# Eight edits to a four-block network kernel: opening, position rounds, band, group norm, one drain

## The reference

```python
# block 0: attention in 14 x 14 windows with relative positions, then an MLP
qkv = win.reshape(Bw, N, C) @ qkv_w + qkv_b              # q, k, v, 12 heads of 16
attn = einsum('bqc,bkc->bqk', q * scale, k)
rel_h = einsum('bhwc,hkc->bhwk', r_q, rel_pos_h[idx])    # the position rounds
rel_w = einsum('bhwc,wkc->bhwk', r_q, rel_pos_w[idx])
out = softmax(attn + rel_h + rel_w) @ v @ proj_w + proj_b
x = x + out; x = x + gelu(_ln(x) @ fc1_w + fc1_b) @ fc2_w + fc2_b
# block 1: group norm, then a Fourier mixer
g = x.reshape(B, H, W, 32, C // 32)
m, s = mean(g, (1, 2, 4)), var(g, (1, 2, 4)); v = (g - m) / sqrt(s + 1e-5)
x = x + irfft2(softshrink(softshrink(rfft2(v) * w1 + b1) * w2 + b2)) + v
# block 2: landmark attention with a 33-tap convolution of v along the tokens,
#          then each token through 2 of 8 experts
# block 3: full attention, then each token through 1 of 8 experts
```

## Time and profile before

| | us |
|---|---|
| runs shown | 1159.53, 1156.06, 1154.65; median 1156.06 |
| profiled execution | 1155.44 |
| its span | 1153.6, mean granted TensorE clock 0.913 |
| PE busy | 998.3 (87%) |
| PE weight loads | 757.4 (66%) |
| DVE, ACT, POOL busy | 578.9, 420.4, 286.6 |

### The profile page before, as it was taken

One profiled execution on the slowest core, in us unless ns is written; L12 is line 12 of the kernel. 1 busy time (PEld: TensorE's weight loads), 2 busy tenths in 40 slices (PEclk: granted clock), 3 DMA queues, 4 the chain that ended last, 5 costly groups with the idle time before them and its releaser, 6 DMA issues. The chain is left out here.

```text
span 1153.6 us, 20446 instructions
## 1 busy us (share of the span) xinstructions
PE 998.3 (87%) x7506; PEld 757.4 (66%) x7507; DVE 578.9 (50%) x1394; ACT 420.4 (36%) x853; POOL 286.6 (25%) x399
## 2 busy tenths in 40 slices
PE   6896999999699699899799839999929789993996
PEld 5685778787466488688699715666727545562775
DVE  3754554653311376465575654444448477844221
ACT  3665054546232133244352101111107356651332
POOL 4464320110100112100000262555422311103242
PEclk9885899999799899899998859999969899995899
DMA  8444863330002120200003711111133433415660
GB/s 92 118 120 122 163 159 81 81 82 2 1 28 71 43 63 2 55 1 1 2 1 84 227 34 30 49 48 49 40 109 90 124 118 99 141 54 173 201 204 15
DMA packets 103318, 91.58 MB, mean 79 GB/s; under 512 B 25905, under 2 KB 95095, under 8 KB 102590
## 3 DMA queue, kind: packets, MB, share of 16 engines
q1 hardware_dynamic: 93161, 77.15, 25.3%
q0 software_dynamic: 5632, 11.07, 3.6%
q10 hardware_dynamic: 4437, 2.17, 0.7%
HBM read 64.44 MB, written 29.70 MB: 82 GB/s over the span
## 5 line engine op out<-in xcount | busy, mean ns | idle before, releaser
L1305 DVE TENSOR_REDUCE l0a_nmax<-l0a_psS 98x2 f32<-98x392 f32 x96 | 54.4, 567 | 54.8 <-PE l0a_psS L1120 50.7
L2743 ACT ACTIVATE l2e_H<-l2e_psH 128x512 f32<-128x512 f32 x40 | 21.7, 594 | 130.2 <-PE l2e_psH L2705 130.2
L895 ACT ACTIVATE l3a_PT<-l3a_psST 128x512 f32<-128x512 f32 x96 | 54.6, 595 | 32.2 <-PE l3a_psST L806 31.4
L1255 ACT ACTIVATE l0a_PT<-l0a_psST 98x392 f32<-98x392 f32 x96 | 47.2, 497 | 42.2 <-PE l0a_psST L1162 41.9
L2723 PEld LDWEIGHTS l2e_psY<-W2T,l2e_HT 128*128 128x128 f32 x320 | 51.5, 190 | 15.9 <-issue 15.8
L2666 POOL DMA_INDIRECT ys<-l2e_Y,result_of x40 | 42.0, 1049 | 72.3 <-DVE l2e_Y L2770 66.2
L2723 PE MATMUL l2e_psY<-W2T,l2e_HT 128*128 x320 | 57.3, 332 | 1.3 <-DVE l2e_Y L2770 0.8
L941 DVE TENSOR_REDUCE l3a_nmax<-l3a_psS 128x2 f32<-128x512 f32 x48 | 33.0, 687 | 25.2 <-PE l3a_psS L776 25.2
L2770 DVE COPY l2e_Y<-l2e_psY 128x384 f32<-128x384 f32 x20 | 11.2, 558 | 65.2 <-PE l2e_psY L2723 65.2
L2702 PE MATMUL l2e_psH<-W1T,l2e_XT 128*128 x80 | 41.3, 640 | 2.7 <-issue 2.0
L2661 POOL DMA_INDIRECT l2e_X<-xn,token_at x40 | 39.3, 981 | 17.1 <-issue 17.1
(11 more groups left out here) (570 smaller groups left out, 2739.6 us busy)
## 6 DMA issues: line engine op xcount, KB each, us to landing
l3w_A<-in_w SPq DMA_DIRECT2D x8, 771.0 KB, 4.6
l3w_B<-in_w SPq DMA_DIRECT2D x8, 672.0 KB, 5.4
l3a_QS<-qd SPq DMA_DIRECT2D x72, 64.0 KB, 2.2
l3a_KS<-kd SPq DMA_DIRECT2D x72, 64.0 KB, 2.3
rd<-l0q_r_p SPq DMA_DIRECT2D x24, 168.0 KB
l0a_QS<-qd SPq DMA_DIRECT2D x54, 64.0 KB
l0a_KS<-kd SPq DMA_DIRECT2D x54, 64.0 KB
W2T<-in_w2t SPq DMA_DIRECT2D x2, 1536.0 KB, 16.7
```

Source lines behind the costliest of these rows:

```text
L895: nc.scalar.activation(PT[n % 3][:, s, :], psST[item % 2][:, :], ACT.Exp).then_inc(exp_done, 1)
L1255: ex = nc.scalar.activation(PT[n % 3][0:WQ, s, :], psST[item % 2][0:WQ, 0:2 * W0], ACT.Exp)
L1305: mx = nc.vector.tensor_reduce(nmax[k % 2][0:WQ, 2 * j:2 * (j + 1), s], psS[item % 2][0:WQ, 0:2 * W0].rearrange("p (t k) -> p t k", t=2), ...
```

## The change

1. Opening: the clearing of `band` and the scatter leave SP's stream for window attention's (after load(4) and load(5)); the six reads of `kb` go from ahead of image 0 to behind image 2.
2. Position rounds: ACT and DVE empty the banks of round r + 1 before they split round r.
3. The position rows of the first group are loaded in the opening.
4. The six products of window attention's start go; three like them stand at the end of the opening, behind the last second piece.
5. Group norm of the first pair: computed inside the MLP by a new `FourierFront`, with the weights of the Fourier mixer loaded at the MLP's start, constant rows behind p = 0, negation behind p = 1, total to square at p = 2, and variance to norm at p = 3.
6. The two-expert block ends without GpSimd's drain; its input semaphores move to the stage around it.

```diff
-    def block(self):
-        return self.ctx.enter_context(self.nc.Block())
+    def block(self, drained=True):
+        return self.ctx.enter_context(self.nc.Block(no_gpsimd_drain=not drained))
 ...
             # opening, SP
             sp.dma_start(rows(G["kbd"], ...), kbp[:, :, :], ...).then_inc(kb_out, 16)
-            sp.dma_start(rows(G["band"], 0, [P * TW, NH], ...), rows(consts["zeros"], ...)).then_inc(band_out, 16)
             sp.dma_start(KOH[:, :], consts["koh"]).then_inc(first_in, 16)
             sp.dma_start(RS[RR:RM, :, :], rows(consts["winrows"], ...)).then_inc(first_in, 16)
-            sp.wait_ge(kb_out, 16)
-            for t, piece in enumerate(K_TERM):
-                sp.dma_start(kb[t * HD:(t + 1) * HD, :], rows(G["kbd"], ...), ...).then_inc(kb_in, 16)
             for i in range(B):
                 for pieces, dst in ((qp, G["qd"]), (kp, G["kd"])):
                     pieces.sync(sp, rows(dst, ...), i, i % 2)
-                if i == 0:
-                    sp.wait_ge(rev_done, 1)
-                    sp.wait_ge(band_out, 16)
-                    sp.dma_start(rows(G["band"], 0, [P * TW, NH], [TW + 1, P], [1, TAPS]), free(backwards[:, 0:1], ...)).then_inc(band_out, 16)
+                if i == 2:
+                    sp.wait_ge(kb_out, 16)
+                    for t, piece in enumerate(K_TERM):
+                        sp.dma_start(kb[t * HD:(t + 1) * HD, :], rows(G["kbd"], ...), ...).then_inc(kb_in, 16)
 ...
                     rp.sync_each(sp, to, *piece_of(r, u))
+                    if (r, u) == (2, 0):
+                        sp.wait_ge(rp.out[0], 2 * rp.unit)
+                        sp.wait_ge(rp.out[2], 2 * rp.unit)
+                        position_rows(sp, G, RS, 0, first_in)
             # opening, TensorE, after the rounds
+            pe.wait_ge(rp.p1, FOURS * len(rounds))
+            for c in range(3):
+                nc.tensor.matmul(psR[:, :], G["ident"][0:CH, :], QF[:, 0, c * 2 * T:(c + 1) * 2 * T], start=True, stop=True)
             # opening, ACT (DVE alike, with its own banks)
-            for r, a, axis in rounds:
+            def relative_out(r, a, axis):
                 if r >= 2:
                     act.wait_ge(rp.rest, FOURS * (r - 1))
                 for bank in (0, 2):
                     act.wait_ge(full[bank], r + 1)
                     evacuate_rel(...).then_inc(emptied[bank], 1)
+            relative_out(*rounds[0])
+            for r, a, axis in rounds:
+                if r + 1 < len(rounds):
+                    relative_out(*rounds[r + 1])
                 ready = [(emptied[bank], r + 1) for bank in range(5)]
                 for u in range(FOURS):
                     rp.scalar(nc, act, columns(axis, u), *piece_of(r, u), *(ready if u == 0 else ()))
 ...
             # window attention, SP and TensorE
-                sp.dma_start(RS[slot][0:RR, :, :], rows(G["rd"], ...)).then_inc(stack_in[slot], 16)
                 if k:
+                    position_rows(sp, G, RS[slot], k, stack_in[slot])
 ...
+                if k == ring:
+                    sp.dma_start(rows(G["band"], ...), rows(G["consts"]["zeros"], ...)).then_inc(band_out, 16)
+                if k == ring + 1:
+                    sp.wait_ge(band_out, 16)
+                    sp.dma_start(rows(G["band"], ...), free(G["backwards"][:, 0:1], ...)).then_inc(band_out, 16)
             early.finish(sp)
+            sp.wait_ge(band_out, 32)
 ...
-            for c in range(6):
-                nc.tensor.matmul(psS[0][:, :], G["ident"][0:CH, :], G["QF"][...], start=True, stop=True)
 ...
             # l0_mlp: SP, POOL, TensorE, ACT, DVE
+            gn.load_weights(sp, w_next)
+            gn.clear_weights()
+                if p == 1:
+                    gn.negate_weights(pool)
+                if p == NP - 2:
+                    pe.wait_ge(xT_done, 2 * NP)
+                    gn.mean(pe, psT[0], 0)
+                if p == NP - 1:
+                    gn.variance(pe, psT[1], 0)
                 second(p)
+                if p == NP - 2:
+                    gn.square(act, 0)
+                    gn.square(act, 1)
+            gn.root(act, 0)
+                if p == NP - 2:
+                    gn.total(dve, 0, (x_in, 16))
+                    gn.centre(dve, psT[0], 0)
+                if p == NP - 1:
+                    gn.square_total(dve, 0)
+                    gn.with_eps(dve, psT[1], 0)
+                    gn.scale(dve, 0)
+                    gn.norm(dve, 0)
+                if p == 0:
+                    gn.constant_rows()
 ...
             # experts_any
-        x_in = [st.sem(f"x_in{r}") for r in range(RING)]
-        y_out = rows_out
+        x_in, y_out = rows_in, rows_out
-        block = st.block()
+        block = st.block(drained=False)
```

More of the change, by code:

```diff
@@ L382, in _ @@
                     pieces.sync(sp, rows(dst, i // 2 * 3 * C * 2 * T + i % 2 * T, [2 * T, CH], [2 * C * T, 3], [2 * CH * T, 2], [1, T]), i, i % 2)
-                if i == 0:
-                    sp.wait_ge(rev_done, 1)
-                    sp.wait_ge(band_out, 16)
-                    sp.dma_start(rows(G["band"], 0, [P * TW, NH], [TW + 1, P], [1, TAPS]), free(backwards[:, 0:1], [0, P], [1, TAPS])).then_inc(band_out, 16)
+                if i == 2:
+                    sp.wait_ge(kb_out, 16)
+                    for t, piece in enumerate(K_TERM):
+                        sp.dma_start(kb[t * HD:(t + 1) * HD, :], rows(G["kbd"], piece * C, [1, HD], [HD, NH]), allow_slow_non_contiguous=True).then_inc(kb_in, 16)
             qp.finish(sp)
@@ L1108, in score @@
                 q_, k_, r_, ps = QS[k % ring][0:SR], KS[k % ring][0:SR], RS[k % ring], psS[item % 2]
[L1109 to L1110 removed]
+                if j == 0 and s == 0 and k:
+                    pe.wait_ge(stack_in[k % ring], 13 * 16 * (k // ring + (1 if k % ring else 0)))
                     if k == 1:
@@ L1648, in backward @@
                 mm.then_inc(y_mm, 1)
-            mean(0)
-            variance(0)
             for p in range(NP):
@@ L1655, in _ @@
                 if p + 1 < NP:
-                    mean(p + 1)
+                    gn.mean(pe, psM, p + 1)
                 first(2 * p)
@@ L1730, in centre @@
-            def centre(p):
-                dve.wait_ge(mean_mm, p + 1)
-                for u in range(2):
-                    V.tensor_tensor(in_groups(XC[u][:]), in_groups(X(2 * p + u)), spread(psM[:, u * GROUPS:u * GROUPS + 1]), ALU.subtract).then_inc(xc_done, 1)
-            def square_total(p):
-                if p:
-                    dve.wait_ge(var_mm, p)
-                for u in range(2):
-                    dve.wait_ge(sq_done, 2 * p + u + 1)
-                    V.tensor_reduce(squares[:, u, :], by_group(SQ[u][:, 0, 0:1]), AX.XY, ALU.add).then_inc(square_done, 1)
@@ L1758, in norm @@
-            def norm(p):
-                for u in range(2):
-                    i = 2 * p + u
-                    if p:
-                        dve.wait_ge(f_mm, 2 * i - 2)
-                        dve.wait_ge(xs_done, i - 1)
-                    V.tensor_tensor(in_groups(XN[u][:]), in_groups(XC[u][:]), spread(rstd[:, u, 0:1]), ALU.mult).then_inc(xn_done, 1)
             def hidden(i, a):
@@ L1812, in _ @@
                 if p + 1 < NP:
-                    total(p + 1)
-                    centre(p + 1)
-                    square_total(p + 1)
+                    gn.total(dve, p + 1, *([(x_in, 16)] if p + 1 == NP - 1 else []))
+                    gn.centre(dve, psM, p + 1)
+                    gn.square_total(dve, p + 1)
                 hidden(2 * p, 0)
@@ L3296, in build @@
         net.window_attention()
-        net.window_mlp()
-        net.fourier()
+        with Stage(nc, "l1g") as across:
+            gn = FourierFront(across, net.G)
+            net.window_mlp(gn)
+            net.fourier(gn)
         net.landmark_attention()
         with Stage(nc, "l2y") as between:
-            rows_out = [between.sem(f"rows_out{r}") for r in range(RING)]
-            net.two_experts(rows_out)
+            rows_in, rows_out = ([between.sem(f"{name}{r}") for r in range(RING)] for name in ("rows_in", "rows_out"))
+            net.two_experts(rows_in, rows_out)
             with Stage(nc, "l3f") as across:
```

241 lines of the change are left out of this document (130 added, 111 removed).

## The result

| | median us | executions | ratio to before, 95% interval |
|---|---|---|---|
| before | 1156.58 | 1154.65 to 1159.53 (4) | |
| changed kernel | 1168.90 | 1166.17 to 1174.91 (4) | 1.0117 [1.0089, 1.0145] |

A forecast was written before the change was run, and what follows sets the result against it. TensorE, busy 998.3 of 1153.6 us, was taken as the bound, through earlier starts or full clock. Six terms summed to −18.5 us from 1155.44, giving 1136.9, then 1137.5 against the runs' median; range 1127 to 1147.

The forecast's parts named there:

- The start of window attention: Window attention: without six products scores start with the stage, group 1 waits for copies to about 8.9 us; −6.4 us.
- Rival (d): Window attention: cold TensorE start, first groups wait on and off, clock stays at half; 1167.5 us, slower; 4%.
- rival (a): Position rounds: new order costs nothing, as TensorE keeps full clock and pieces overlap; 1132 us; 15%.
- The images: Opening: band transfers and kb copies no longer delay qd, so the slow image pair becomes like the fast one; −7.7 us.
- The rounds: Position rounds: round 2's units wait behind VectorE's round 3 copies, and piece 7 for piece 4's buffer; +7.4 us.
- The band in window attention: Window attention: clearing of band holds SP's queue, so load(5) lands after its scores are due; +3 us.
- Rival (c): Window attention: band transfers hold loads by the full +8 us and the clock falls in that wait; 1144.5 us; 12%.
- The group norm: MLP and Fourier stage: first pair's norm moves into the MLP, so forward products start sooner and run faster; −9.8 us.
- The drain: End of two-expert stage: without GpSimd's drain the barrier waits only for the last indirect transfer's issue; −5.0 us.
- Rival (b): After the two-expert stage: drain only moves, as the next stage's reads of ys wait for the same transfers; 1142.5 us; 10%.

The follow-up runs named there:

- e5: e3 with six products instead of three at the opening's end and none at window attention's start: 1143.04, 1156.31, 1168.40 and 1174.72 us.
- e2: The kernel before without its six products at window attention's start, nothing else: 1180.97, 1191.17, 1207.78 and 1210.05 us beside 1155.24.
- e1: The changed kernel with the six products put back at window attention's start: 1142.87 us beside 1155.24, ratio 0.9890.
- e3: e1 with the old order of the position rounds (banks emptied right before the round is split): 1133.58 us beside 1155.24, ratio 0.9828.
- e4: The changed kernel with only the old order of the position rounds, still without the six products: 1165.23 and 1165.68 us beside 1155.24.
- e7: e3 without the three products at the opening's end, six kept at window attention's start: 1132.75 us beside 1154.91.
- e12: e3 with the six reads of kb back ahead of image 0, band transfers still in window attention: 1143.23 us beside 1157.31.
- e15: e3 with the clearing of band and the scatter in the opening instead of window attention: 1142.86 us beside 1155.75.
- e18: e16 with the clearing of band and the scatter behind window attention's last load too: median 1132.31 us beside 1156.15.
- e9: e5 with three products added at the start of window attention: 1130.15 to 1158.09 us, median 1146.85, beside 1157.31.
- e10: e5 with three products added at the wait for group 1's copies: 1134.82 to 1144.87 us, median 1137.86, beside 1157.31.
- e8: e3 with GpSimd's drain back at the end of the two-expert block: 1140.10 us beside 1154.91.
- e16: e10 with the sixteen weight and constant transfers behind window attention's last load instead of load(3): 1130.34 us beside 1156.15, ratio 0.9775.
- e13: e10 with the sixteen weight and constant transfers behind load(5) instead of load(3): 1147.28 us beside 1155.75.

## Why the prediction was wrong, step by step

The predicted 1137.5 us was missed by 31.4. Five of the six terms came within 3 us of the traces; the sixth turned a gain of 6.4 into a loss of 27.7.

- **The start of window attention (−6.4): the step that failed.** It took the six products for 8.3 us of work that nobody reads, let "up to a quarter more for a cold clock" hide in the wait for group 1's copies, and went on at full clock behind it. In the changed kernel group 0 took 13.1 us at half clock (120.30 to 133.36) instead of 7.0, with no wait in it to hide in. Where the stage did start at full clock (e5), group 1's scores began 9.8 us behind its start, near the 8.9 of the term: what failed is the clock, not the copies. The runs show that the scores and products of this stage, at half clock, need not raise it at all: 85.7 us in the changed kernel, at least 120 in e2, while TensorE is busy without a break. The same instructions at full clock keep it (e1, e3). The six products are what carries TensorE from the one to the other. The three products left in the opening do not. In the changed kernel they ran at half clock to their end and 2.9 us of idle time followed; in e4 the clock rose within them and was lost again over 3.7 us of idle time; beside the six they change nothing (e7).
- **Rival (d) is what happened, in the main.** A cold start and a clock that stays at half, in this stage and at this kind of price, were right; that the first groups "wait on and off" was not, as TensorE did not wait at all. The stretch was 86 us and not 60, so that its 1167.5 lies 1.4 from the measured time is partly luck. Its chance of 4% was a misjudgement. The evidence stood in the earlier trace rows: TensorE busy 5.40 of 5.40 us at a clock of 0.62. Finer windows of the same stretch show that this mean is a fall:

```profile
74.00:76.30 2.30, 2.30 (x22) 2.15 (x21) 0.98 (x6) 0.03 (x1) 2.24 (x2) 0.99 0.72 187
76.30:80.40 4.10, 4.10 (x23) 4.10 (x22) 3.04 (x4) 3.68 (x4) 2.23 (x2) 0.50 0.19 49
```

TensorE had been busy without a break since 58.9, and yet the clock fell at 76.3, 6.8 us after the position rounds began (69.50). So here busy time alone neither lifts the clock nor keeps it; rival (a) has the words for it ("the clock fell while TensorE was busy"), but they were not carried over to (d). I set against it that the clock was at 1.00 behind the six products, which is no evidence for a kernel without them. The Trainium skill's "activity releases the throttle" (page "TensorE: Matmul & The Clock Gate", Part 1) did not help here, as 85.7 us of continuous recorded activity did not release it.
- **The images (−7.7).** −6.9 in the slow pair, −6.2 at the rounds' start (69.50 to 63.34). Right, but for one reading: the band clearing was not what held the queue (e12).
- **The rounds (+7.4).** +8.2 in the traces, 7.4 between e1 and e3, by the predicted path: piece 7 waits for the buffer of piece 4. Rival (a) is out: TensorE ran its last round at half clock (5.29) as before.
- **The band in window attention (+3).** 0 (e15, e18). The 14.6 us in the opening, from which the term was made, were another transfer's wait (e12), so the base of the estimate was wrong; its lower bound held. Rival (c) falls with it, though its clock part, a wait for copies that drops the clock, is just what e5, e9 and e10 showed once the stage started earlier.
- **The group norm (−9.8).** −9.1 between the traces before and after, and 1.68 us of waiting for `psT` where 1.3 was expected.
- **The drain (−5.0).** −5.8 by the gap behind the last transfer, 6.5 by e8's traces. Rival (b) is out.

The forecast without its failed term, −18.5 + 6.4 = −12.1, stands beside e1's measured −12.4. That it comes so near is luck in part: the band term was 3.0 too high, the images' gain 1.5 too large and the rounds' price 0.8 too low. Three sums in the working are slightly off, without effect on the outcome: 6.6 − 0.4 + 2.1 to 2.5 is 8.3 to 8.7 and not 8.9, 1.3 + 0.3 is 1.6 and not 1.7, and the bounds add in squares to −6.7 and +8.4 and not to ±5, which the stated range still covers. The terms but one were sound; what failed was to take instructions without a reader for instructions without an effect. The prediction had even priced it: "From 2 × 18.5 = 37 us at half the whole gain is gone".

## What to carry to other kernels

Before products whose result nobody reads are taken out, look at the granted clock ahead of and behind them: if it rises within them, their price is their duration, and their worth about half of the TensorE-bound time that would run at half clock without them. A warm start (a stage that begins at full clock) has to survive each idle time up to steady work, so after speeding up a stage's start look for the next wait for a transfer; a weight prefetch ahead of a working load in the same queue can cause one. And take several executions: a kernel that sits between the two levels of the clock shows it first as spread.

The kernel with the lowest median here, e16, moves the sixteen transfers behind the last load, has six products at the end of the opening and three at group 1, and the old order of the rounds: 1130.34 us, 2.2% under the kernel before. The simpler e3 is 1.7% under it, three of its four executions lie within 0.2 us, and the intervals of the two ratios overlap.

## What the runs showed of the hardware that was not expected

- Two lasting clocks at the same work. In window attention TensorE's stream ran for 85.7 us (changed kernel) and 120 us (e2) at 0.50, and in e1 from 126 us to the end of the stage at 1.00. The product ahead of the rise is no fixed one; in the changed kernel the clock rose at 206.7 us and in e4 at 200.4, 86.4 and 87.5 us behind the stage's start, in e2 at 246.4, 128 us behind it.
- The clock can fall without any idle time: at 76.3 us in the kernel before, TensorE had been busy since 58.9.
- How little goes with a loss of it: a wait of 2.1 us in e5, and in e16 no wait longer than the 1.1 us at the barrier; in the profiled execution of e18 a wait of 1.0 us at the same place did not lose it.
- Sixteen transfers ahead of a load made TensorE wait for that load for 2.8 to 3.4 us in one place (e10, e9) and for 8.0 in another (e13); with them behind the last load (e16) no such wait was left.
- SP waited 13.4 us for a write of 1.1 KB (e12), without the 960 KB clearing behind it that the prediction held to be the reason.
